# A fused attention, delta-rule and expert kernel: VectorE's and TensorE's loops get other boundaries

## What is computed

```python
x = x + _L0_xattn_ref(_layernorm(x, axis=-1), ctx_768, ...)
x = x + _L0_attn_ref(_layernorm(x, axis=-1), ...)
x = x + _L0_ffn_ref(_layernorm(x, axis=-1), ...)
```

```python
def step(S, inp):
    k_t, q_t, v_t, beta_t, a_t = inp
    S = S * a_t[..., None, None]
    kv_mem = jnp.einsum('bhd,bhde->bhe', k_t, S)
    delta = (v_t - kv_mem) * beta_t
    S = S + k_t[..., :, None] * delta[..., None, :]
    y_t = jnp.einsum('bhd,bhde->bhe', q_t, S)
    return (S, y_t)
```

## Time and profile before

| what | value |
|---|---|
| median of 3 runs | 3303.29 us (3297.47 to 3306.33) |
| the profiled execution's own time | 3298.92 us |
| its span, first to last instruction | 3296.9 us |
| mean granted TensorE clock | 0.969 of 2.4 GHz |
| busy: TensorE, VectorE, ScalarE, GpSimd | 94%, 61%, 41%, 19% |

### The profile page before, as it was taken

How to read it: one execution, slowest core, us unless ns; L and a number is a source line. 1 busy time by engine, 2 the same in 40 slices (tenths; PEclk the granted TensorE clock), 3 DMA queues, 4 the chain that set the end, 5 groups by cost and what they waited for, 6 DMA issues and landing times. The chain is left out here.

```text
span 3296.9 us, 87695 instructions
## 1 busy us (share of the span) xinstructions
PE 3106.4 (94%) x35570; PEld 2274.9 (69%) x35570; DVE 2007.4 (61%) x4107; ACT 1336.0 (41%) x3360; POOL 642.1 (19%) x514
## 2 busy tenths in 40 slices
PE   6999999999999999999999999999999788898995
PEld 5777777777777777777777777777777555544542
DVE  3333366756766677567666675766676487893323
ACT  3444444444444444444444444444443233322321
POOL 0011111111111111111111111111111276601334
PEclk9999999999999999999999999999999898899997
DMA  4222322232223222222222222222321688535479
GB/s 167 69 73 86 102 95 80 88 101 84 81 79 97 84 80 80 97 89 80 79 97 84 84 84 97 84 81 79 101 85 64 148 252 258 175 131 164 136 265 329
DMA packets 297853, 378.10 MB, mean 115 GB/s; under 512 B 159568, under 2 KB 211536, under 8 KB 296016
## 3 DMA queue, kind: packets, MB, share of 16 engines
q1 hardware_dynamic: 287184, 338.19, 32.3%
q0 software_dynamic: 10240, 33.56, 2.9%
HBM read 258.17 MB, written 189.01 MB: 136 GB/s over the span
## 5 line engine op out<-in xcount | busy, mean ns | idle before, releaser
L120 PE MATMUL ring<-cond_high,wkv_high 128*128 128x342 f32 (+1 forms) x1152 | 406.0, 352 | 57.0 <-issue 20.0
L120 PE MATMUL ring<-cond_low,wkv_high 128*128 128x342 f32 (+1 forms) x1152 | 373.2, 324 | 0.0
L120 PE MATMUL ring<-cond_high,wkv_low 128*128 128x342 f32 (+1 forms) x1152 | 371.9, 323 | 0.0
L615 ACT ACTIVATE shared_rows<-ring,kvb 128x342 f32<-128x342 f32 (+1 forms) x384 | 209.4, 545 | 381.4 <-PE ring L120 381.4
L840 DVE TENSOR_REDUCE neg_max<-score 128x4 f32<-128x1028 f32 x128 | 157.3, 1229 | 289.0 <-PE score L947 289.0
L120 PE MATMUL ring<-wkv_high,cond_high 128*128 128x512 f32 x768 | 316.6, 412 | 0.0
L169 DVE TENSOR_TENSOR prod<-coef,deltas 128x64 f32<-128x64 f32 (+30 forms) x248 | 308.7, 1245 | 5.9
L120 PE MATMUL ring<-wkv_high,cond_low 128*128 128x512 f32 x768 | 303.0, 395 | 0.0
L120 PE MATMUL ring<-wkv_low,cond_high 128*128 128x512 f32 x768 | 302.8, 394 | 0.0
L120 PEld LDWEIGHTS ring<-cond_high,wkv_high 128*128 128x128 f32 x1152 | 220.4, 191 | 107.6 <-issue 54.7
L649 ACT ACTIVATE prob<-score,neg_max 128x257 f32<-128x257 f32 x512 | 235.9, 474 | 135.6 <-DVE neg_max L840 135.6
(11 more groups left out here) (199 smaller groups left out, 5502.9 us busy)
## 6 DMA issues: line engine op xcount, KB each, us to landing
cond<-cond_t_dram SPq DMA_DIRECT2D x128, 385.5 KB, 4.2
xs<-slot_rows SPq DMA_DIRECT2D x78, 256.0 KB, 2.8
slot_rows<-ys SPq DMA_DIRECT2D x78, 256.0 KB, 2.0
x_rows<-x SPq DMA_DIRECT2D x64, 256.0 KB, 2.7
vb_rows<-vgb SPq DMA_DIRECT2D x64, 256.0 KB, 3.5
x_in<-x_dram SPq DMA_DIRECT2D x32, 256.0 KB, 3.2
kk_rows<-kk_rows_s SPq DMA_DIRECT2D x32, 256.0 KB, 2.7
qk_rows<-decay SPq DMA_DIRECT2D x32, 256.0 KB, 2.8
```

The source lines that it names most:

```text
L120: last = pe.matmul(out, lhs_t, rhs, start=start and i == 0, stop=stop and i == len(terms) - 1)
L615: act.activation(k_t[:, group, at:at + n], ring_bank[bank][:, 0:n], ACT.Identity, bias=kvb[:, group:group + 1]).then_inc(ring.free[bank], 1)
```

## The change

In VectorE's program the end of a turn becomes a function of its own, `turn_end`, and is called in front of the next turn. The order of VectorE's instructions stays; the loop now begins in front of the wait for the projection and ends behind the last `low_terms`. In TensorE's program turn 1 is written out and the loop has two turns in each of its 15 rounds, turns 2 to 31. Lines behind the new function's head move down by two, so L873 becomes L875.

```diff
@@ -869,6 +869,8 @@
                 if more:
                     low_terms(u + 1, BU - 1)
 
+            def turn_end(u):
+
                 dve.wait_ge(proj_ready, u + 1)
                 dve.tensor_tensor(x1[:], turned[1][:], x1[:], ALU.add).then_inc(x1_ready, 1)
                 dve.wait_ge(x1_ready, u + 1)
@@ -879,15 +881,18 @@
                 low_terms(0, b)
             turn(0)
             for u in range(1, LAG):
+                turn_end(u - 1)
                 turn(u)
             before, per_group = own.n, GU * 14 + 3 * (N - 1) + sum(len(folds(t)) for t in range(N))
             with dve.Fori(0, NG - 2) as group:
                 own.turn(before, group, per_group)
                 for quarter in range(GU):
+                    turn_end(group * GU + (LAG + quarter - 1))
                     turn(group * GU + (LAG + quarter), group, quarter)
                 assert own.n == per_group, own.n
             own.turn(before + (NG - 2) * per_group, 0, 0)
             for quarter in range(GU):
+                turn_end(NU - GU + quarter)
                 turn(NU - GU + 1 + quarter, NG - 2, quarter, last=(quarter == GU - 1))
 
         @block.tensor
@@ -1080,8 +1085,10 @@
 
             turn(0, first=True)
             pe.wait_ge(attn_loaded, 16 * 6)
-            with pe.Fori(1, NU) as u:
-                turn(u)
+            turn(1)
+            with pe.Fori(1, NU // 2) as pair:
+                turn(pair * 2)
+                turn(pair * 2 + 1)
             turn(NU, last=True)
```

## The result

The changed kernel takes 3310.79 us (median of 19 runs, 3304.64 to 3330.67), the kernel before, run beside it, 3302.6 us: a ratio of 1.0034 [1.002, 1.0047]. It is slower by just over what can be told from no change. I had forecast 3293 us and faster, and gave "slower" a chance of 0.15.

The account below looks back on a forecast made before the run. TensorE, busy 94% of the span, was taken as the bound; 24.7 + 8.9 - 24.4 + 1 = 10.2 us off the profiled 3298.9 gave 3288.7, or 3293 us at the median. Range 3254 to 3314, the forecast's own 3280 to 3314.

Parts of the forecast that it names:

- VectorE's boundary: VectorE's five jumps move into its 6.63 us wait for the projection, covering both late pages: 24.7 us gained.
- TensorE, jumps removed: TensorE's jumps in front of unit 2 and the odd units 3 to 31 go: 8.9 us gained.
- Unit 31: Removing TensorE's jump here gains nothing, since TensorE waits 3.33 us for VectorE's `q_s` in the last two turns anyway.
- TensorE, the jumps left: Jumps before even units 4 to 28 land with four matmuls left: 3.4 us each, 44.2 against 19.8, 24.4 us lost.
- jump and landing: Price of a cheap TensorE jump in front of an even unit: 0.5 us.
- idle behind the matmuls left: TensorE's four matmuls end at +0.9 us, the second page serves at +2.8: 2.0 us idle a jump.
- half clock: TensorE at half clock behind a jump's stop, taken as half of 1.8 us: 0.9 us a jump.
- Unit 30: TensorE's jump in front of it costs nothing, being under the 3.33 us wait for `q_s`, so 13 of 14 count.
- Second pass: Moves by 162 in TensorE's pages; between 2 us lost and 4 gained, taken as 1 us gained.
- rival "slower": TensorE's second page as late as VectorE's: 4.64 us idle and half clock each jump, 13 x 6.9, 3340 us; chance 0.11.
- The rival by which all jumps are cheap: TensorE's landing page lasts because the count of places is off by a few tens: gain 46.9, 3256 us; chance 0.27.

Follow-up runs that it names:

- landing at 248: VectorE's new loop boundary with TensorE's old loop of single turns, plus 74 idle instructions at the head of TensorE's program: 3373.1 us, a single run.
- the kernel of the 16 idle instructions: The changed kernel with 16 idle instructions at the head of TensorE's program: 3260.27 us, 0.9864 of the kernel before.
- run 127: Not a follow-up run but a verb and a count: in the kernel before, TensorE's y stage had run 127 matmuls, then 128 and 128, between stalls.
- the new boundary in its bad place: The changed kernel with 16 idle instructions on TensorE and 8 on VectorE, which lands some four instructions ahead of a page's end: 3253.98 us, 0.9838.
- the kernel without a jump: VectorE's new loop boundary with TensorE's turns 1 to 31 all written out, against the kernel before: 3259.15 us, 0.9849.

## Why the prediction was wrong

**VectorE's boundary: right.** Forecast -24.7 us over the five stretches; measured -27.4, of which 2.5 are the jumps of TensorE that I had counted under the next head. The stop at BN_STATS is covered and the second page costs nothing. With VectorE's half alone the five sum to 393.00, 5 x 78.60. What I had not seen is that 2.85 us of lateness were free in any case: moving the boundary is one of two ways to the same gain.

**TensorE, jumps removed: right.** Forecast 8.9 us with those in the five; measured 8.2 without them. Unit 31 gave nothing, as said.

**TensorE, the jumps left: this step failed, in its size.** Forecast 3.4 us for each of 13; measured 1074.15 - 13 x 78.07 = 59.2, 4.6 each. Its three terms:

| term | forecast | measured |
|---|---|---|
| jump and landing | 0.5 | 0.3 (the rest) |
| idle behind the matmuls left | 2.0 | 2.4 (31.1 in 13) |
| half clock | 0.9 | 1.8 |

The place was five instructions out, two matmuls left instead of four; the next page served at +3.0 us against my +2.8, so the idle time is 0.4 longer, 5 us in 13. The larger error is the clock. I took half the jumps to bring 3.4 us of half clock, since stops of up to 1.9 us had done so in two of nine and those of 2.2 and more in five of five, and 2.0 lay between. Twelve of thirteen brought it (two of them 6.8 us; at 1.7 us lost for each 3.4, 23.8 us). The row of unit 28 shows the stop without it: 80.79, 2.7 over 78.07, clock 1.00. The thirteen cost 39.0 us more than before instead of 24.4, 14.6 too much: 12 of it are the clock, 5 the idle time, less 2 for cheaper landings. The second profile of the changed kernel and the one with TensorE's half alone had half clock in 14 of 14 and 13 of 14, so it was no accident of this execution. A sharp bound is not to be had from the runs: landing at 248, eight of 28 stretches kept the full clock behind stops of the same 2.0 to 2.6 us.

**Unit 30: this step was wrong in kind.** I let its jump cost nothing, "under that same cover", TensorE's 3.33 us wait for `q_s`. The wait is still there, whole, and 4 us later. VectorE's timeline in this unit, first before the change (TensorE's lines are five further down in the changed kernel, so L996 is L1001):

```profile
2424.42 0.17 DVE L764 TENSOR_TENSOR z<-score,dtb 128x16 f32<-128x16 f32 x1
...
2438.77 0.17 DVE L780 COPY square<-score 128x16 f32<-128x16 f32 x1 [0.19 <-PE score L996]
...
2453.74 0.69 DVE L834 SCALAR_TENSOR_TENSOR q_s<-ring,qb_scaled 128x512 f32<-128x512 f32 x1
```

and in the changed kernel, with TensorE's wait behind it:

```profile
2428.28 0.17 DVE L764 TENSOR_TENSOR z<-score,dtb 128x16 f32<-128x16 f32 x1 [2.31 <-PE score L120]
...
2444.24 0.17 DVE L780 COPY square<-score 128x16 f32<-128x16 f32 x1 [1.79 <-PE score L1001]
...
2459.21 0.69 DVE L834 SCALAR_TENSOR_TENSOR q_s<-ring,qb_scaled 128x512 f32<-128x512 f32 x1
```
```profile
2460.05 1.12 PE L1055 MATMUL ring<-wattn,x1n_t 128*128 128x512 f32 x2 [3.32 <-DVE q_s L834]
```

`q_s` begins 44.5 us behind the unit's addition before and 48.5 after. VectorE, full in this unit, waits 2.31 and 1.79 us for TensorE's alpha and Gram products, which the stop and 6.8 us of half clock made late. The waits go round in a ring, TensorE to VectorE to TensorE, and a stop ahead of the first link is not covered: `q_s` is 4.0 of the 5.5 us. A wait for another engine covers a stop only if that engine's work does not itself depend on what the stop delays.

The other 1.5 us are clock behind the wait for `q_s`: half for some 3.4 us, where it stayed whole before. This part does not need the stop: the kernel of the 16 idle instructions has none, and its unit 30 lasts, with half clock for some 6.8 us behind a wait of 3.57 us for `q_s`,

```profile
2366.24:2451.44 85.20, 81.02 (x928) 61.79 (x929) 59.31 (x112) 35.70 (x93) 10.65 (x9) 0.96 0.24 79
```

So 3.8 of the 89.0 us go with the stop. In all thirteen other profiled executions unit 30 has a clock of 0.94 to 0.98; the one of the kernel before, 1.00, was the exception, and I built on it.

**Second pass:** forecast 1 us gained; the time behind the last addition changed by -0.5. The page ends moved, by 176 places and not by my 162: the y stage ran 167, 128 and 89 matmuls, where it had run 127, 128, 128 and then one more behind a third stop. First that one, then the changed kernel:

```profile
2631.25 0.26 PE L1603 MATMUL y<-shared_rows 32*32 32x32 f32 x1 [2.09 <-issue]
...
2623.01 2.37 PE L1610 MATMUL y<-shared_rows 32*32 32x32 f32 x167 [7.92 <-PEq L222]
2627.73 1.85 PE L1610 MATMUL y<-shared_rows 32*32 32x32 f32 x128 [2.35 <-issue]
2635.04 1.40 PE L1610 MATMUL y<-shared_rows 32*32 32x32 f32 x89 [5.46 <-issue]
```

That is 7.8 us of stops against 8.8, so this stage did gain the 1 us. Across the kernels here this pass took 713 to 727 us with the same work; I did not find out why, and 1 us cannot be told from it.

**In sum** the landing place and its mechanism were right, and the forecast's -10.2 us became +6.4 by three terms: 14.6 us more of clock and idle time in the thirteen, 5.5 in unit 30, less 3.5 gained elsewhere. The rival "slower" was to decide from 4.1 us a jump, and it was 4.6, but not as that rival had it: it took 4.64 us of idle time and half clock at every jump, 6.9 in all. The clock was the rival's, the idle time, 2.4 us, nearly the forecast's 2.0. The price of 4.6 lies inside the forecast's own range of 2.3 to 4.9 a jump, and above the 4.1 at which the gain is gone; the forecast of a gain rested on 3.4.

The rival by which all jumps are cheap, 3256 us, is what the same code does when it lands elsewhere: 3260 and 3254 us. The Trainium skill (Runtime: NRT & Kernel Launch, Instruction fetch mechanics) says "Prefetch is purely sequential"; the one packet more a jump agrees. It also has the crossing from page to page "mostly hidden"; here that holds with 40 matmuls left (the kernel before) and not with ten. The prediction took its 2048 instructions for the window in which a jump is free; the section speaks of a "current 2-page window", by which the old body, over seven pages long, pays for its jumps too, and the ten packets a unit agree.

## What to carry to other kernels

Before a loop's shape is judged, count where its jump lands: with a few instructions left in the page, the engine stops until the next one is there, and here that decided between 0.4% slower and 1.4% faster for the same loop. Lengthening a body, or writing a turn out, moves all landings behind it; a few idle instructions ahead of the loop move them back, and VectorE's jump, put inside a wait that was there anyway, cost nothing in a good place and in a bad one. Price a stop with the clock that it brings down, and only call it covered when the other engine's work doesn't itself wait for what it delays.

## What the runs showed of the hardware

- TensorE used the page behind the landing page about 3 us after the landing (2.6 to 3.4 us behind the unit's first matmul), with 2, 3 or 10 matmuls left; a landing with room cost 0.5 to 0.7 us (the even stretches with 16 idle instructions are 78.9 on average, the odd ones 78.2).
- Behind a stop of 0.9 to 1.5 us the granted clock stayed at 1.00 in all 28 stretches of units 2 to 29; behind 2.1 to 2.8 us it fell to half in 13 of 14 with the change (14 of 14 and 13 of 14 in two more runs with that landing), and behind 2.0 to 2.6 in 20 of 28 landing at 248. But in single stretches it also fell without a stop at the jump, as in 1345.29 to 1425.13 (79.84 us, clock 0.98) with the new boundary in its bad place, and in unit 4 of the kernel without a jump (79.85 us, 0.98). In both the half clock began some 27.7 us into the stretch, just behind the 128 small products of 32x64; why there, and why so seldom, is not shown.
- What idle instructions cost at a program's head cannot be told: with 88 of them on TensorE the first addition came at 95.97 us instead of 89.28, or at 92.38 instead of 89.40, with 60 at 89.08. It is paid once, if at all.
